# First attention of a two-layer block: q, k and v projected by halves, and the gates of all heads computed at once and loaded as a band per head

## What is computed

```
h = layernorm(x) * (1 + scale) + shift                 # per batch, from the modulation of c
q = conv4(h @ Wq); k = conv4(h @ Wk); v = conv4(h @ Wv); z = h @ Wz   # per head, 256 -> 128
# each conv: silu, then a causal 4-tap filter over the tokens; q and k rotated and normalised
a = h @ Wa; b = h @ Wb                                  # one number per token and head
gate[t, u] = sigmoid(a[t] * b[u])                       # of a key t and a query u, 0 <= u - t < 4
o[u] = sum over t of (q[u] . k[t]) * gate[t, u] * v[t]
y = rmsnorm(o * silu(z)) @ Wout
```

## Time and profile before

| what | us |
|---|---|
| three runs of before | 1248.58, 1257.54, 1256.71 (median 1256.71) |
| the profiled execution, its own time | 1249.32 |
| its span in the profile | 1247.5 |
| of the span: TensorE busy | 1091.8 (88%) |
| VectorE, ScalarE, GpSimd busy | 759.9, 554.3, 264.9 |

### The profile page before, as it was taken

One profiled execution on the slowest core, in us unless ns is written; L12 is line 12 of the kernel. 1 busy time (PEld: TensorE's weight loads), 2 busy tenths in 40 slices (PEclk: granted clock), 3 DMA queues, 4 the chain that ended last, 5 costly groups with the idle time before them and its releaser, 6 DMA issues.

```text
span 1247.5 us, 16995 instructions
## 1 busy us (share of the span) xinstructions
PE 1091.8 (88%) x5693; PEld 779.3 (62%) x5693; DVE 759.9 (61%) x1332; ACT 554.3 (44%) x1256; POOL 264.9 (21%) x228
## 2 busy tenths in 40 slices
PE   6989999999999979947977999999998967329996
PEld 4666667666766664423436999988985425128885
DVE  1497788878887858963136778787772034303344
ACT  1266767676766648920014555655551002002320
POOL 0032223222222220012002111111100000546660
PEclk9799999999999978978988999999998987759997
DMA  6055445643555330060001110111001000148854
GB/s 266 19 143 138 100 95 140 129 110 95 128 132 145 78 101 1 1 185 1 0 0 52 52 50 26 50 50 50 25 0 51 1 13 1 76 161 262 271 170 178
DMA packets 51349, 110.50 MB, mean 89 GB/s; under 512 B 7827, under 2 KB 30558, under 8 KB 50544
## 3 DMA queue, kind: packets, MB, share of 16 engines
q1 hardware_dynamic: 41584, 84.32, 20.9%
q0 software_dynamic: 9728, 25.72, 10.4%
HBM read 69.52 MB, written 27.89 MB: 78 GB/s over the span
## 4 chain that ended last, share of the span: by engine, by line
PE 41%; DVE 12%; issue 4%; POOL 3%; ACT 2%; DMA 1%; DVEq 0%; POOLq 0%; ACTq 0%; SPq 0%
PE psum L709 5%; PE psum L611 4%; PE psum L797 4%; PE psum L512 4%; PE psum L490 3%; PE psum L492 3%; PE psum L491 3%; PE psum L682 3%; PE psum L807 2%; DVE arena L1197 2%; POOL slot_rows L1514 2%; PE psum L628 2%; PE psum L249 1%; DVE lut_w L1197 1%; PE psum L786 1%
## 5 line engine op out<-in xcount | busy, mean ns | idle before, releaser
L1090 DVE SCALAR_TENSOR_TENSOR arena<-arena,par_in 128x1024 f32<-128x1024 f32 x144 | 184.7, 1284 | 52.5 <-ACT arena L870 38.3
L512 PE MATMUL psum<-h_t,arena 128*128 128x512 f32 x384 | 174.0, 597 | 0.0
L512 PEld LDWEIGHTS psum<-h_t,arena 128*128 128x128 f32 x384 | 69.3, 190 | 73.2 <-issue 73.2
L611 PE MATMUL psum<-G,arena 128*128 128x512 f32 x256 | 112.6, 602 | 2.7 <-DVE G L1289 1.5
L961 ACT ACTIVATE arena<-psum,small 128x256 f32<-128x256 f32 x128 | 59.2, 472 | 85.8 <-DVE small L1237 85.7
L611 PEld LDWEIGHTS psum<-G,arena 128*128 128x128 f32 x256 | 49.3, 193 | 64.8 <-issue 64.8
L1469 POOL TENSOR_TENSOR small<-small 128x16 f32<-128x16 f32 x16 | 46.8, 2928 | 199.5 <-DVE small L1116 199.5
L860 ACT ACTIVATE arena<-psum 128x1024 f32<-128x1024 f32 x48 | 49.3, 1026 | 83.4 <-PE psum L512 83.4
L490 PE MATMUL psum<-arena_r 128*128 128x256 f32 x256 | 77.7, 303 | 1.5 <-DVE arena_r L1262 1.5
L1475 POOL DMA_DIRECT2D arena<-arena x64 | 53.9, 983 | 117.4 <-DVE arena L1102 117.2
L286 POOL TENSOR_TENSOR small<-small 128x8 f32<-128x8 f32 x6 | 9.9, 1642 | 321.7 <-DVE small L277 305.7
(11 more groups left out here) (194 smaller groups left out, 2357.2 us busy)
## 6 DMA issues: line engine op xcount, KB each, us to landing
arena<-arena POOLq DMA_DIRECT2D x64, 256.0 KB, 7.6
arena<-in_w_moe SPq DMA_DIRECT2D x32, 384.0 KB, 3.8
slot_rows<-nowhere SPq DMA_DIRECT2D x16, 576.0 KB, 4.9
arena<-slot_rows SPq DMA_DIRECT2D x32, 288.0 KB, 3.9
arena<-in_w_qkvz SPq DMA_DIRECT2D x16, 512.0 KB, 3.8
arena<-b_rows SPq DMA_DIRECT2D x16, 512.0 KB, 9.0
arena<-in_qkv_codes SPq DMA_DIRECT2D x16, 384.0 KB, 3.2
arena<-in_qkv_scales SPq DMA_DIRECT2D x64, 96.0 KB, 3.0
```

What stands on the lines that cost most here:

```text
L512: i = nc.tensor.matmul(dst[0:rows, n * 512:n * 512 + 512], w(k), h_t[:, k * T + n * 512:k * T + n * 512 + 512], start=(k == 0), stop=(k == ...
L611: i = nc.tensor.matmul(bank(2 * m + n), w[:, h * D + m * P:h * D + m * P + P], G[:, h * T + n * 512:h * T + n * 512 + 512], start=(h == 0) ...
L1090: nc.vector.scalar_tensor_tensor(by_batch(dst), by_batch(u[s])[:, :, j:j + S], par_in[:, bass.ds(M_CW + (w * H + h) * TAPS + j, 1)], by_ba ...
```

## The change

**Projections.** q, k and v of each head are projected by halves as in the second attention: 12 MATMUL records of fp32r take the place of 8 of f32. z stays f32. The upper half of h (`hh_h`) and the lower (`hh_l`) are made once before the turns. The halves of the weights are made per head: ScalarE copies 768 columns to fp32r (`upper0(h + 1)`, after the k tap of turn h), VectorE subtracts (`lower0(h + 1)`, after the `rows_sb` copy of turn h), and the q projection of head h+1 waits for it.

**Gates.** a and b of all heads are transposed at four lags (32 transposes instead of 8), multiplied for all heads, passed through one tanh of 512 columns, and scaled by a table `lags`. Per head SyncE scatters 128 x 8 pieces of 4 floats onto the diagonals of a zeroed 128 x 1056 array in DRAM (two such arrays, in turn) and loads that array whole as the band (540 KB). The eight tanh per turn and the gate instruction of VectorE go, and so does the row load. The band is 132 wide per tile.

**Rest.** The table's indices are loaded after the last turn's z projection; `wout` waits for the rotations. Before the turns two zero fills of the DRAM arrays are issued. One more pair of turns is written out instead of looped, since the last turn prepares no weights.

```diff
-                    project(slot(0), lambda k: w(0, k), P).then_inc(sg("a0_q"), 1)
+                    pe.wait_ge(sg("a0_w_lo"), h + 1)
...
+                def project0(dst, j):
+                    for n in range(2):
+                        for k in range(KC):
...
+                            i = by_halves(dst[:, n * 512:n * 512 + 512], w_hi[par][:, w], w_lo[par][:, w], hh_h[:, c], hh_l[:, c],
+                                          k == 0, k == KC - 1)
...
+                    project0(slot(0), 0).then_inc(sg("a0_q"), 1)
...
+            pe.wait_ge(sg("ba_sb"), 2)
+            for s in range(TAPS):
+                for t in range(NT):
+                    i = nc.tensor.transpose(lag_block(s)[:, t * 2 * H:t * 2 * H + 2 * H], ba_sb[:, t * P + s:t * P + s + P],
...
+            act.wait_ge(sg("gate_args"), 1)
+            nc.scalar.activation(gates, gates, ACT.Tanh).then_inc(sg("gate_tanh"), 1)
+            def upper0(h, hh, par):
+                act.wait_ge(sg(f"a0_w{par}"), 16 * (hh + 1))
+                if since(h, 2):
+                    act.wait_ge(sg("a0_v"), h - 1)
+                nc.scalar.activation(w_hi[par], wh[par][:, 0:QKV], ACT.Copy).then_inc(sg("a0_w_hi"), 1)
...
-                    for i in range(NT):
-                        n = P if i % 2 else WIDE
-                        m = nc.scalar.activation(gate[:, i * WIDE:i * WIDE + n], b_all[:, i * P:i * P + n], ACT.Tanh,
...
+            def lower0(h, par):
+                dve.wait_ge(sg("a0_w_hi"), h + 1)
+                nc.vector.tensor_tensor(w_lo[par], wh[par][:, 0:QKV], w_hi[par].bitcast(F32), ALU.subtract)\
+                    .then_inc(sg("a0_w_lo"), 1)
...
-                    nc.vector.scalar_tensor_tensor(by_tile(gm, WIDE), by_tile(gate, WIDE), 1.0, over_tiles(band, NT),
-                                                   ALU.add, ALU.mult).then_inc(sg("a0_gm"), 1)
...
                     nc.vector.tensor_copy(rows_sb[0:2 * NT, :], bank(7)[0:2 * NT, 0:P]).then_inc(sg("a0_rows_sb"), 1)
+                if 4 in st:
+                    lower0(h + 1, 1 - par)
...
+            def scatter(h, par):
+                c = bass.ds(h * NT * TAPS, NT * TAPS)
+                sp.dma_start(diagonals(par), by_tile(gates[:, c], TAPS)).then_inc(sg(f"a0_lags{par}"), 16)
...
+                    scatter(h + 1, 1 - par)
+                if since(h, 2):
+                    sp.wait_ge(sg("a0_A"), h - 1)
+                sp.wait_ge(sg(f"a0_lags{par}"), 16 * (hh + 1))
+                sp.dma_start(gm[par], bands[par]).then_inc(sg(f"a0_band{par}"), 16)
```

More of the change, by code:

```diff
@@ L20 @@
 PAD = TAPS - 1
-WIDE = P + PAD
+WIDE = P + TAPS
 BAND = NT * WIDE
@@ L115, in build @@
         strict = cst[:, C_STRICT:C_STRICT + P]
-        band = cst[:, C_MASK:C_MASK + WIDE]
+        half_scale, seam = 0.5 * SCALE, cst[:, C_SEAM:C_SEAM + PAD]
         cos_t, sin_t = cst[:, C_COS:C_COS + S], cst[:, C_SIN:C_SIN + S]
@@ L134, in build @@
         rqk = [rqk0, rqk1]
-        ss_all = few(H * NT)
+        ss_all, lags = few(H * NT), few(NT * TAPS)
         nmax, rsum, rinv = few(8), few(8), few(8)
@@ L167, in build @@
         lut_v, lut_b0 = [lv0, lv1], [lb0.bitcast(I32), lb1.bitcast(I32)]
-        (wout,) = carve(H * D, base=3 * UW + 14 * T + PAD + 2 * BAND + P)
+        (wout,) = carve(H * D, base=3 * UW + 11 * T + TAPS + 3 * BAND + P + H * NT * TAPS)
         hsb = [hsb0, hsb1]
@@ L337, in turns0 @@
         def turns0(eng, turn):
-            turn(0, 0, 0, (1,))
-            turn(1, 0, 1, (1, 2))
-            with eng.Fori(1, H // 2) as i:
-                turn(2 * i, i, 0, (1, 2, 3))
-                turn(2 * i + 1, i, 1, (1, 2, 3))
+            turn(0, 0, 0, (1, 4))
+            turn(1, 0, 1, (1, 2, 4))
+            with eng.Fori(1, H // 2 - 1) as i:
+                turn(2 * i, i, 0, (1, 2, 3, 4))
+                turn(2 * i + 1, i, 1, (1, 2, 3, 4))
+            turn(H - 2, H // 2 - 1, 0, (1, 2, 3, 4))
+            turn(H - 1, H // 2 - 1, 1, (1, 2, 3))
             turn(H, H // 2, 0, (2, 3))
@@ L394, in _ @@
             sp.wait_ge(sg("pool_fill"), 1)
+            for par in range(2):
+                sp.dma_start(by_tile(bands[par], WIDE), over_tiles(nil[:, 0:WIDE], NT)).then_inc(sg("bands_nil"), 16)
+            sp.wait_ge(sg("bands_nil"), 32)
+            sp.wait_ge(sg("gates"), 1)
+            scatter(0, 0)
             turn(0, 0, 0, True)
@@ L921, in turn @@
                             act.wait_ge(sg("a0_g_hi"), h)
-                        m = nc.scalar.activation(junk[:, i * P:i * P + P], slot(1)[:, i * P:i * P + P], ACT.Square, scale=rqk[1 - par][:, i:i + 1],
+                        m = nc.scalar.activation(v_tok[:, i * P:i * P + P], slot(1)[:, i * P:i * P + P], ACT.Square, scale=rqk[1 - par][:, i:i + 1],
                                                  accum_out=ss_all[:, bass.ds((h - 1) * NT + i, 1)])
                     m.then_inc(sg("a0_sqo"), 1)
+            for k in range(KC):
+                act.wait_ge(*norm("n0", "out", k))
+                nc.scalar.activation(chunk(hh_h, k), chunk(h_t, k), ACT.Copy).then_inc(sg("in_hi"), 1)
+            upper0(0, 0, 0)
             turns0(act, turn)
```

114 lines of the change are left out of this document (68 added, 46 removed), and 2 rows, old and new, of the table REUSED.

## The result

| | median us | runs | ratio to before, 95% interval |
|---|---|---|---|
| before, same chip | 1250.82 | 8 | |
| changed kernel | 1263.7 | 8 | 1.0088 [1.006, 1.0116] |
| its profiled execution | 1264.09 (span 1262.3) | 1 | |

The forecast was 1264. The changed kernel is 12.9 us slower at the median, 14.8 us between the two profiled executions. By the ratio it is 11.0 us (0.0088 of 1250.82), and its interval goes from 7.5 to 14.5. Ratios here leave out the few executions in a slower state (one each of e1_lower_early, e14_pool_scatter2 and before), which the medians contain, and they are not quotients of the medians (that would be 1.0103 here).

What follows compares the result with a forecast made beforehand. TensorE, busy all 25.16 us of a turn, bounds the kernel, VectorE's loop just under it. Terms 9.3 + 7.0 - 3.0 - 0.9 - 1.2 = 11.2 us slower give 1260.5 or 1267.9; forecast 1264 between, range 1248 to 1281.

Steps and rivals of the forecast that it cites:

- The mechanism: Middle turns: TensorE's work falls to 23.3 us, but its 1.9 us saving becomes a wait of about 1.8 us behind lower0.
- The start: Before the first q projection: a chain over three engines that nothing hides makes head 0 start 9.3 us later.
- The chain of six steps: Start: 32 transposes, gate products, tanh, upper halves, lower halves, then lower0(0), putting the first q at 58.7 instead of 49.36.
- Turn 0 and turn 1: First two turns: turn 0 now waits for VectorE, 7.0 us more; turn 1 gets 3.0 us shorter.
- Turn 1 ... now it is a turn of 25.09: Turn 1 took 28.08 us while TensorE caught up on VectorE; now 25.09, 3.0 us less.
- The middle turns: Turns 2 to 14: 25.09 us each against 25.16, a gain of 0.07 a turn and 0.9 us over 13 turns.
- first filter to the copy: 18.22 ... all in between stays: VectorE's stretch of a middle turn, from first filter to copy, was to stay at 18.22 us.
- The end: Last turn, which prepares no weights: head 14's transposes come 1.6 us earlier; taken as -1.2 us, from -1.6 to +3.
- Rival 1: TensorE stays the bound and the gain is real: turns of 23.3 us, 20 us faster, 1229 to 1237; chance 0.07.
- Rival 2: The scatter's 1024 small pieces delay the rotation DMAs: 1.5 us a turn, 21 us in all, 1281 to 1289; chance 0.10.
- The old row load is gone: Argument that the scatter would not delay the rotation DMAs: the earlier row load no longer shares the engines; no size given.
- Rival 3: The new 1.8 us gap at the head of each turn lowers TensorE's clock, up to 1280; chance 0.03.

Runs made afterwards that it cites:

- e1_lower_early: Changed kernel with VectorE's weight subtraction lower0 moved from behind the copy to right behind the scores' multiplication; ratio to before 1.0004.
- e14_pool_scatter2: Changed kernel with the weight subtraction on GpSimd and every scatter made twice, the second to an array nobody reads; ratio to before 0.9998.
- e15_shift_only: Changed kernel with scatter, band load and fills issued after the scores' multiplication, next weights behind them; subtraction stays last on VectorE; ratio to before 1.0094.
- e3: Changed kernel with the weight subtraction of heads 1 to 15 on GpSimd instead of VectorE (also called e3_lower_pool); ratio to before 1.0033.
- e8_shift: Changed kernel with subtraction on GpSimd, and scatter, band load and fills issued after the scores' multiplication, weights last; ratio to before 0.9937.
- e4_start: Changed kernel with the halves of h and of head 0's weights made before the gates instead of behind them; ratio to before 1.002.
- e5_scatter2: Changed kernel with every scatter made twice, the second to an array nobody reads; ratio to before 1.0094.
- e2_gates_only: Changed kernel with q, k and v projected in f32 as before, without halves, so only the gates' change remains; ratio to before 1.012.
- e10_gates_no_scatter: Kernel of e2_gates_only with the 16 scatters left out, so the gates are left out of the result; ratio to before 1.0109.

## Why the prediction was right, and where it was off

**The mechanism was the one on record.** TensorE's work fell to 23.3 us a turn (23.24 in turns without waits), and the saving turned into a wait at the head of the turn behind `lower0`. Predicted was about 1.8 us; it was 1.53 at 363.43 and 1.44 to 1.57 in turns 2 to 14 of e15_shift_only, where late rotation DMAs hardly disturb it. Moving that instruction (e1, e3) takes the wait away, and moving the transfers without it (e15) leaves it. e15_shift_only and e8_shift differ in the place of this instruction alone, with ratios of 1.0094 and 0.9937. That shows the cause of the wait by runs.

**The start: 9.3 against 9.0.** The chain of six steps held, and e4_start shows that it is a matter of order: 6.9 of it go if the halves are made first.

**Turn 0 and turn 1: +7.0 and -3.0 against +7.4 and -2.3.** The failing step is "Turn 1 ... now it is a turn of 25.09". TensorE had no work of stages 2 and 3 in turn 0, so it stood for 6.42 us before q of turn 1 and restarted at a clock of 0.72. I had charged the lower clock to turn 0 only.

**The middle turns: -0.9 against -3.8.** The step that was mis-sized is "first filter to the copy: 18.22 ... all in between stays". It took 387.14 - 369.10 = 18.04. All of this difference lies ahead of the k filters: now they start 373.26 - 369.10 = 4.16 us after the first filter, and before it was 357.44 - 353.10 = 4.34, by these rows of VectorE's timeline before:

```profile
357.18 0.17 DVE L1116 TENSOR_SCALAR small<-psum 128x16 f32<-128x16 f32 x1
357.44 4.14 DVE L1090 SCALAR_TENSOR_TENSOR arena<-arena,par_in 128x1024 f32<-128x1024 f32 x3
```

The small instruction had ended at 357.35, so VectorE stood 0.09 us even there; now the next filter starts without that gap, which fits the shorter k projection. The turn's sum is then 3.18 + 2.49 + 18.04 + 0.20 + 0.99 = 24.90. Turns 2 to 13 take 24.95 on average, 0.14 under the forecast, 1.7 us in all twelve.

The other 1.05 us are turn 14 alone: from q at 413.37 to q at 437.41 it takes 24.04. It is the turn that is now written out instead of looped, and the prediction put that at nothing without a reason. In it VectorE's filters run closer together, three in 3.93 us instead of 4.14, and first filter to copy takes 436.10 - 418.72 = 17.38:

```profile
418.72 3.93 DVE L1158 SCALAR_TENSOR_TENSOR arena<-arena,par_in 128x1024 f32<-128x1024 f32 x3 [2.48 <-ACT arena L914]
...
436.10 0.27 DVE L1202 COPY arena<-psum 16x128 f32<-16x128 f32 x1
```

Turn 14 of e15_shift_only is as short (23.91), and turn 0 before, written out too, has six of these filters in 7.77 us. Why a looped turn is slower on VectorE no run tests. My estimate from these rows is that, while VectorE's chain sets the turn, writing a turn out is worth some 1 us.

**The end: -1.2 against -2.4,** below its range (-1.6 to +3). The transposes of head 14 come 463.48 - 437.41 = 26.07 us after the last q start instead of 28.09, 2.0 us earlier where 1.6 were forecast, and the way from them to the out-projection is 0.4 us shorter too, although the scores of head 15 wait 1.86 us for the rotation DMAs. No run tests it alone.

The terms' sum was 11.2; measured from transposes to out-projection it is 8.0. The 12.9 us at the median hold some 5 us that none of my terms names; by the ratio it is 3, and 8.0 lies inside its interval (7.5 to 14.5), so these us may be noise. Of the 14.8 between the profiled executions, 4.7 are the later start of the transposes, which scatters by itself, and 2.1 lie behind the first attention. The 1264 also stood on 1252.8 for the kernel before, which then measured 1250.82, so that two misses cancelled. The forecast's closeness, 0.3 us, is luck; what was right is the mechanism and the sum within some 3 us.

**Rival 1** (the gain is real) was rightly rejected, and e8_shift is that rival built, by two more edits: some 8 us faster than before by the ratio (0.9937).

**Rival 2** was half right. The scores do wait for the rotation DMAs (10 times, 8.0 us in all), but under the wait for VectorE, and so they cost the changed kernel nothing in its turns. Its mechanism was wrong: doubling the 1024 pieces of 16 B changed neither kernel, and leaving out the band load cured it (leaving out the scatter did too, most likely because the band load then comes earlier). "The old row load is gone" stood in my text as a reason against this rival. It should have been the other way round: a load of the same size came back, and what counted was that SyncE now issues it into the rotation DMAs instead of behind them. The rule of the Trainium skill that I weighed (DMA: Bandwidth & Descriptors, Specifications), that pieces below 512 B become read-modify-writes, may hold for each piece, and the scatter of 16 KB does land in 8.1 us at the median; but the runs show no charge of it to the DMAs beside it.

**Rival 3** (the gap lowers the clock) does not show in the turn listed, with its 1.53 us and a clock of 1.00. But it happened in two turns of e15_shift_only and one of e5_scatter2 after waits of the same length (1.45 to 1.53 us), at some 1.5 us each.

**What stays open.** e2_gates_only and e10_gates_no_scatter cost 1.2% and 1.1% with turns of nearly the old length. From the transposes to z they take 4.8 us longer than before: 1.9 are the later q, 2.9 the lower clock. The first q ran at 0.50 to 0.51 in e2_gates_only, e10_gates_no_scatter and e4_start, straight after 32 transposes, and at 1.00 in the one profile of before, after 8. No run varies the number of transposes alone, so that these are the cause is not shown. The rest of the 13 us is not assigned.

## What to carry to other kernels

When the engine that is full is relieved, ask at once which engine's chain is just under it (here VectorE's, busy for 20.9 of 25.2 us), and put none of the new work at its end: a single 0.95 us instruction at the tail of VectorE's turn held 1.1 us of each turn (24.9 in most turns of e15_shift_only against 23.8 in e8_shift), and on GpSimd, which had room, the wait for it was gone. A large load that is needed a turn later still has a time at which it must not be issued; the row load was harmless behind the rotation DMAs, the band load ahead of them, and in the midst of them it cost 1 us a turn (24.97 against 23.93 and 23.96) once nothing hid it. Work that feeds only a later step (the gates) should not stand ahead of what the first product waits for.

## What the runs showed of the hardware

- Another 1024 pieces of 16 B per turn, from the chip's own memory to DRAM, on SyncE's queue cost no measurable time (1.0094 against 1.0088, and 0.9998 against 1.0033 where late rotation DMAs are not hidden), while without the one load of 528 KB behind them the GpSimd queue's DMAs land 2.1 us earlier at the median (6.0 against 8.1).
- The median landing was a poor guide here: at 8.6 us (e8_shift) the scores waited 6.1 us in all, at 8.1 (e3_lower_pool) 16.2. The maximum, 10.8 against 12.8, went with the waits.
- GpSimd's power of 16 columns took 3.84 us on average instead of 2.93 (line 1534 after, 1469 before), on the same shape. It is 2.93 too in e2_gates_only and e10_gates_no_scatter, which project in f32, and 3.78 to 3.84 in every run that projects by halves. So it goes with the projections or the work of making halves, not with the gates; the reason is not shown.
- VectorE's three filter instructions took 4.14 us in a looped turn and 3.93 in a written-out one (turn 14, 418.72), on the same shapes.
- With the subtraction on GpSimd (1.82 us there, 0.94 on VectorE), VectorE's rotation product that starts during it took 1.67 instead of 1.22 us:

```profile
341.72 1.82 POOL L1535 TENSOR_TENSOR arena_r<-arena,arena_r 128x768 fp32r<-128x768 f32 x1
...
342.95 1.67 DVE L1164 TENSOR_TENSOR arena<-arena,cst 128x1024 f32<-128x1024 f32 x1
```
